# Two graph-attention layers on one core: layer 2 takes layer 1's tile scheme, and its normalization moves from POOL to DVE and ACT

## What is computed

```python
def _gat_layer(h, mask, b):
    scores = jnp.einsum('...nd,...md->...nm', h, h)
    scores = jnp.where(mask, scores, NEG)
    attn = jax.nn.softmax(scores, axis=-1)
    return jnp.einsum('...nm,...md->...nd', attn, h) + b
...
out_h = _gat_layer(h, mask[None, None], bh[None, :, None, :])      # H = 4 heads
z = jax.nn.leaky_relu(cat, negative_slope=0.2)
h2 = jnp.einsum('bnk,dk->bnd', z, Wo)
out2 = _gat_layer(h2, mask[None], bo)
z2 = jax.nn.leaky_relu(out2, negative_slope=0.2)
mu = jnp.mean(z2, axis=-1, keepdims=True)
var = jnp.mean(jnp.square(z2 - mu), axis=-1, keepdims=True)
out = (z2 - mu) * jax.lax.rsqrt(var + LN_EPS) * gamma + beta
...
x = _layernorm(x + _L1_gnn_ref(...), axis=-1)
```

## Time and profile before

| | |
|---|---|
| Median of three runs | 3392.47 us (3391.7 to 3395.71) |
| The profiled execution | 3385.7 us |
| Its span, first to last instruction | 3384.0 us |
| Mean granted TensorE clock | 0.964 |
| PE busy | 3073.0 us (91%) |
| DVE busy | 2755.6 us (81%) |
| ACT busy | 2336.7 us (69%) |
| POOL busy | 2600.1 us (77%) |

### The profile page before, as it was taken

The page is one execution under the profiler, slowest core; times in us unless marked ns, Lnnn a source line. Parts: engine busy times, 40 slices in busy tenths (PEclk is TensorE's granted clock), DMA queues, the critical chain, the costliest instruction groups (busy, mean ns, idle before and its releaser), DMA issues. The chain is left out here.

```text
span 3384.0 us, 126835 instructions
## 1 busy us (share of the span) xinstructions
PE 3073.0 (91%) x49399; PEld 2298.0 (68%) x49399; DVE 2755.6 (81%) x5040; ACT 2336.7 (69%) x2678; POOL 2600.1 (77%) x1891
## 2 busy tenths in 40 slices
PE   4874679999999999999999999999996599999997
PEld 3433457777777777777777777777765477777775
DVE  5477668888888888888888888888876599999998
ACT  1003557777777777777777777777765488888886
POOL 1026968999999999999999999999986337676775
PEclk7886989999999999999999999999998899999998
DMA  5103679998999999899999999999976623333331
GB/s 204 64 0 124 233 172 159 174 178 161 163 181 171 162 178 176 163 172 179 167 166 175 174 163 175 178 161 167 180 135 202 207 105 142 125 139 130 142 127 72
DMA packets 1195556, 528.52 MB, mean 156 GB/s; under 512 B 1091998, under 2 KB 1149788, under 8 KB 1192988
## 3 DMA queue, kind: packets, MB, share of 16 engines
q1 hardware_dynamic: 1193964, 518.57, 73.0%
q0 software_dynamic: 1200, 3.93, 0.3%
HBM read 123.09 MB, written 62.91 MB: 55 GB/s over the span
## 5 line engine op out<-in xcount | busy, mean ns | idle before, releaser
L627 POOL TENSOR_TENSOR mask_slot<-probs 128x1024 f16<-128x1024 f32 x1024 | 1915.7, 1893 | 209.5 <-ACT probs L984 123.0
L984 ACT ACTIVATE probs<-scores,shifted_max 128x2048 f32<-128x2048 f32 x512 | 1026.1, 2004 | 171.2 <-DVE shifted_max L1191 167.3
L1186 DVE CUSTOM_DVE_ANT_0 scores<-ps,mask 128x1024 f32<-128x1024 f32 x512 | 627.1, 1225 | 259.9 <-PE ps L842 255.3
L841 PE MATMUL ps<-operands 128*128 128x512 f16 x2048 | 778.7, 380 | 15.8 <-DMA v_parts<-h_d 15.1
L842 PE MATMUL ps<-operands 128*128 128x512 f16 x2048 | 778.0, 380 | 0.0
L989 ACT COPY probsT<-ps 128x1024 bf16<-128x1024 bf16 x512 | 518.1, 1012 | 360.9 <-PE ps L850 360.9
L1186 DVE CUSTOM_DVE_ANT_0 scores<-ps,mask,neg_max 128x1024 f32<-128x1024 f32 x512 | 657.4, 1284 | 93.3 <-issue 66.3
L850 PEld LDWEIGHTS ps<-ident,probs 128*128 128x128 bf16 x8192 | 515.8, 98 | 283.8 <-issue 145.9
L850 PE MATMUL ps<-ident,probs 128*128 128x128 bf16 x8192 | 624.2, 219 | 6.8 <-DVE probsT L1195 4.9
L861 PE MATMUL ps<-v_parts,probsT 128*128 128x64 f16 x8192 | 547.6, 193 | 0.0
L860 PE MATMUL ps<-v_parts,probsT 128*128 128x64 f16 x8192 | 547.2, 193 | 0.0
(11 more groups left out here) (171 smaller groups left out, 4640.1 us busy)
## 6 DMA issues: line engine op xcount, KB each, us to landing
mask_slot<-mask SPq DMA_DIRECT2D x129, 512.0 KB, 2.9
operands<-hT_d SPq DMA_DIRECT2D x160, 256.0 KB, 4.1
operands<-hT_d SPq DMA_DIRECT2D x40, 512.0 KB, 4.7
v_parts<-h_d SPq DMA_DIRECT2D x40, 512.0 KB, 5.0
scores<-in_adj SPq DMA_DIRECT2D x16, 1024.0 KB, 4.8
h_d<-outs SPq DMA_DIRECT2D x32, 512.0 KB, 2.8
hT_d<-probs SPq DMA_DIRECT2D x32, 512.0 KB, 2.8
probsT<-mask_slot SPq DMA_TRANSPOSE x1024, 3.9
```

What stands on the lines that cost most here:

```text
L627: pool.tensor_tensor(low[:, u, w], probs[:, u, w], high[:, u, w], ALU.subtract).then_inc(sem(f"low{half}"), 1)
L841: pe.matmul(ps[:, b, :], k_both[:, p, t * P:(t + 1) * P], q_head[:, p, w], start=True, stop=False)
L984: act.activation(probs[:, 1 - u, :], scores[:, 1 - u, :], ACT.Exp, bias=shifted_max[:, 1 - u:2 - u], scale=-1.0, accum_out=row_sum[:, held ...
L1186: dve.tensor_tensor_reduce(scores[:, u, w], ps[:, 2 * c:2 * c + 2, :].rearrange("p a n -> p (a n)"), mask[:, t * N + c * 2 * BANK:t * N + ...
```

## The change

Layer 2 runs through layer 1's step, now called `tile_step`, with `second` true: bf16 high part transposed by PE, low part subtracted on POOL and transposed by DMA, mask read from SBUF directly. `attention`, `step` and the staged mask go. The operands lie in two buffers: `hi_lo` (high above low), which serves as weights too, and `lo_hi` (low above high); this holds for layer 1 as well and makes four DMAs of 1.5 MB together.

The output of layer 2 gets its bias while it is copied, tile by tile. The normalization of instance i-1 and that of i-2 (its second part) run beside instance i, one piece per tile, on DVE and ACT. One chain of Newton steps on DVE at tile 13 makes the roots for both. Beta is added to x1 by POOL in the stage between. SP stores the output. Behind the last tile the pieces of the last two batches run by themselves (`after_layer2`), with the last scalings on DVE.

```diff
-        q_head = operands[:, 0]
-        q_tail = operands[:, 1]
-        k_both = operands[:, 2]
+        hi_lo = operands[:, 0]
+        lo_hi = operands[:, 1]
...
-                if k == 5:
+                if k == 3:
...
-                to, half, part, rows_ = ((q_head, 0, 0, D), (q_tail, 0, 1, D), (k_both, 0, 0, P), (q_head, 1, 0, D), (q_tail, 1, 1, D))[k]
+                to, row, at, rows_ = ((hi_lo, 0, 0, P), (lo_hi, 0, D, D), (lo_hi, D, 0, D))[k]
...
-            sp.dma_start(mask_slot[:, 0, :], mask[:, 0:N]).then_inc(sem("mask_staged0"), 16)
-
-            attention(LAYER1, INSTANCES, sp, step, 2 + OPERAND_DMAS)
...
+            unrolled(sp, tile_step, LAYER1, B)
+            after_layer2(finish)
+            sp.wait_ge(sem("out_stored"), 16 * B)
...
+                if w == 3:
+                    pool.tensor_tensor(by_tile(x1_of(b)), by_tile(x1_of(b)), parameter(3), ALU.add).then_inc(sem("beta_added"), 1)
...
-                            pe.matmul(ps[:, b, :], k_both[:, p, t * P:(t + 1) * P], q_head[:, p, w], start=True, stop=False)
+                            pe.matmul(ps[:, b, :], hi_lo[:, p, t * P:(t + 1) * P], hi_lo[:, p, w], start=True, stop=False)
...
-            attention(LAYER1, INSTANCES, act, step, 4)
+            unrolled(act, tile_step, LAYER1, B)
+            after_layer2(finish)
```

ACT's pieces (`i` is the instance under way, `p` its buffer, `tail` true behind the last tile):

```diff
+                if t == 7 and ends(i - 2):
+                    act.wait_ge(sem("f_centred2"), nth(i - 2))
+                    gate(act, "act")
+                    act.square(scratch2[:, :], x1_of(i - 2 - LAYER1)).then_inc(sem("f_squared2"), 1)
+                if t == 10 and ends(i - 1):
+                    act.wait_ge(sem("f_centred"), nth(i - 1))
+                    act.square(scratch[:, :], outs[:, 1 - p, :]).then_inc(sem("f_squared"), 1)
+                if t >= 14 and ends(i - 1) and not tail:
+                    if t == 14:
+                        act.wait_ge(sem("f_rstd"), nth(i - 1))
+                    scale_tiles(outs[:, 1 - p, :], ln[:, 4, :], *((0, 6) if t == 14 else (6, 11)))
+                if t == 0 and ends(i - 2) and (not tail or i == INSTANCES):
+                    scale_tiles(outs[:, p, :], ln[:, 4, :], 11, 16).then_inc(sem("f_scaled"), 1)
+                if 1 <= t < 4 and ends(i - 3) and (not tail or i == INSTANCES):
+                    scaled = scale_tiles(x1_of(i - 3 - LAYER1), ln[:, 5, :], *((0, 6), (6, 11), (11, 16))[t - 1])
```

DVE's output copy and its pieces, which stand at the end of the tile's step; waits and semaphores of the later ones are cut:

```diff
+                    if second:
+                        for tt in range(4 * k, 4 * k + 4):
+                            added = dve.scalar_tensor_tensor(outs[:, held, tt * D:(tt + 1) * D], out_slot(tt), row_inv[:, held, tt:tt + 1],
+                                                             rows[:, 1, :], ALU.mult, ALU.add)
...
+                if ends(i - 1):
+                    if t == 5:
...
+                        dve.scalar_tensor_tensor(y, y, 0.2, y, ALU.mult, ALU.max).then_inc(sem("f_leaky"), 1)
+                    if t == 8:
...
+                        dve.tensor_reduce(ln[:, 0, :], by_tile(y), AX.X, ALU.add).then_inc(sem("f_sum"), 1)
+                        dve.wait_ge(sem("f_sum"), n)
+                        dve.tensor_scalar(ln[:, 0, :], ln[:, 0, :], -1.0 / D, None, ALU.mult).then_inc(sem("f_mean"), 1)
+                    if t == 9:
...
+                        dve.tensor_tensor(by_tile(y), by_tile(y), over_features(ln[:, 0, :]), ALU.add).then_inc(sem("f_centred"), 1)
+                    if t == 12:
...
+                        dve.tensor_reduce(ln[:, 2, :], by_tile(scratch[:, :]), AX.X, ALU.add).then_inc(sem("f_ssq"), 1)
...
+                if t == 13 and (ends(i - 1) or ends(i - 2)):
+                    inverse_roots(n)
+                if ends(i - 2):
...
+                    if t == 1:
...
+                        dve.tensor_tensor(by_tile(y), by_tile(y), parameter(2), ALU.mult).then_inc(sem("f_gamma"), 1)
+                    if t == 2:
...
+                        dve.tensor_tensor(x1, x1, y, ALU.add).then_inc(sem("f_added"), 1)
+                    if t == 4:
...
+                        dve.tensor_reduce(ln[:, 1, :], by_tile(x1), AX.X, ALU.add).then_inc(sem("f_sum2"), 1)
...
+                    if t == 6:
...
+                        dve.tensor_tensor(by_tile(x1), by_tile(x1), over_features(ln[:, 1, :]), ALU.add).then_inc(sem("f_centred2"), 1)
+                    if t == 10:
...
+                        dve.tensor_reduce(ln[:, 3, :], by_tile(scratch2[:, :]), AX.X, ALU.add).then_inc(sem("f_ssq2"), 1)
...
+                then(dve.tensor_scalar(r.bitcast(I32), v.bitcast(I32), -0.5, 1597463007.0, ALU.mult, ALU.add))
+                for k in range(3):
+                    then(dve.tensor_tensor(newton[:, :], v, r, ALU.mult))
+                    then(dve.tensor_tensor(newton[:, :], newton[:, :], r, ALU.mult))
+                    then(dve.tensor_scalar(newton[:, :], newton[:, :], -0.5, 1.5, ALU.mult, ALU.add))
+                    root = dve.tensor_tensor(r, r, newton[:, :], ALU.mult)
+                    if k < 2:
+                        then(root)
```

More of the change, by code:

```diff
@@ L116, in pair, with unrolled @@
             return ap.rearrange("p (b c) -> p b c", c=D)
[L123 to L152 removed]
+        def unrolled(eng, step, first, count):
+            second = first == LAYER1
             def run(i, p, fresh=False):
@@ new lines, in by_tile, with over_features, parameter, x1_of @@
+        def by_tile(ap):
+            return ap.rearrange("p (t c) -> p t c", c=D)
+        def over_features(ap):
+            return ap.rearrange("p (t o) -> p t o", o=1).to_broadcast([P, NT, D])
+        def parameter(k):
+            return rows[:, k:k + 1, :].to_broadcast([P, NT, D])
+        def x1_of(b):
+            return col(xs, b, NT * D)
+        def ends(i):
+            return not isinstance(i, int) or LAYER1 <= i < INSTANCES
+        def nth(i):
+            return i - LAYER1 + 1
@@ L375, in _, with after_layer2 @@
+        def after_layer2(finish):
+            for t in range(FLUSH, NT):
+                finish(INSTANCES, t, 0, True)
+            for t in range(NT):
+                finish(INSTANCES + 1, t, 1, True)
+            for t in range(6):
+                finish(INSTANCES + 2, t, 0, True)
         @block.sync
@@ L484, in layer1_step, with finish @@
                     load_part(i + 1, 1 - p, k)
-                if t == 10 and not (isinstance(i, int) and i == 0):
+                if t == 10 and not second and not (isinstance(i, int) and i == 0):
                     store_z(i - 1, 1 - p)
+                if second:
+                    finish(i, t % NT, p)
+            def finish(i, t, p, tail=False):
+                if t == 5 and ends(i - 3):
+                    b = i - 3 - LAYER1
+                    sp.wait_ge(sem("f_done"), b + 1)
+                    gate(sp, "sp")
+                    sp.dma_start(out[b].rearrange("(p t) c -> p (t c)", t=NT),
+                                 x1_of(b)).then_inc(sem("out_stored"), 16)
             def load_z(b, w):
@@ L822, in layer1_step, with tile_step @@
-            def layer1_step(g, i, t, p, back):
+            def tile_step(g, i, t, p, back, second):
                 u = t % 2
@@ L989, in layer1_step, with finish, scale_tiles @@
                     act.copy(highT[:, u, N // 2:N], high_bank(1)).then_inc(sem("high_copied1"), 1)
-            unrolled(act, layer1_step)
+                if second:
+                    finish(i, t % NT, p, t >= NT)
+            def finish(i, t, p, tail=False):
+                def scale_tiles(v, rstd, first, end):
+                    for tt in range(first, end):
+                        scaled = act.activation(v[:, tt * D:(tt + 1) * D], v[:, tt * D:(tt + 1) * D], ACT.Copy, scale=rstd[:, tt:tt + 1])
+                    return scaled
+                if t == 7 and ends(i - 2):
[13 more added lines that the diff above has]
+                    scaled = scale_tiles(x1_of(i - 3 - LAYER1), ln[:, 5, :], *((0, 6), (6, 11), (11, 16))[t - 1])
+                    if t == 3:
+                        scaled.then_inc(sem("f_done"), 1)
+            unrolled(act, tile_step, 0, LAYER1)
             def copy_zT(k, u):
```

371 lines of the change are left out of this document (92 added, 279 removed).

## The result

The changed kernel took 3371.82 us (median of 4, 3368.04 to 3374.07) against 3392.09 (3389.44 to 3395.71) for the kernel before: a ratio of 0.9938 [0.9921, 0.9956]. It is 0.6% faster, 20 us. I had forecast 3402 us, 0.3% slower: the sign was wrong, the time inside the range.

A forecast was written before the change was run, and what follows sets the result against it. PE bounded both layers before, with DVE nearly full in layer 2; DVE would set layer 2 afterwards. The terms -5 + 3 - 9 + 7.5 + 2 + 11 = +9.5 us gave 3402 us; range 3325 to 3435.

The forecast's parts named there:

- The start of layer 2: Before layer 2's first mask: lighter operand loads and no wait for the staged mask row, together -9 us.
- The tail: From the last output copied to the end: two whole batches left unfinished, 33 us instead of 22.7, +11 us.
- From the last mask to the last output copied: After the last tile: 11.9 us instead of 9.5, +2 us.
- Instance: 74.8 + 3.4 + 4.4 + 2.2 + 1.2 = 86.0 us: 16 layer 2 tiles: DVE's work, pass waits, Newton's waits, PE's clock loss, two light steps set by PE.
- 661 forecast for layer 2: Layer 2: instances of 65, 81 and six at 86, less 1; against 653.5 before, +7.5 us.
- own range of the forecast: Whole kernel: 3380 to 3425 us, from 83 to 89 us an instance and the ends of other terms; chance 0.6.
- rival 1: Layer 2, tile 13: the waits hardly happen, an instance takes 76 us, the whole about 3335 us, faster; chance 0.25.
- Rival 2: Layer 2: a waiting DVE instruction always waits for both POOL halves, the whole about 3459 us; chance 0.15.
- Rival 3: Layer 1: operand loads were its limit, so -13 us instead of -5, the whole 3394 us; no chance given.
- -5: Layer 1: fewer operand loads shorten PE's wait for transposed data, -5 us (ends 0 and -13).
- -4.2: Start of layer 2: DVE's last copy waits 16.8 us behind operand loads; a quarter less gives -4.2 us.
- The stage between: Between the layers: POOL's eight additions of beta cost +3 us (ends 0 and 16).

The follow-up runs named there:

- two small repairs: Changed kernel with Newton's intermediates in PSUM and beta's additions taken out of the stage between: 3329.78 us, 0.9836 of the kernel before.

## Why the prediction failed

**What held.** DVE, not PE, sets layer 2 and fills 91% of it. The waits are where the text put them: in instructions that read SBUF twice, at tiles 1 to 9, and in Newton's chain at tile 13, with two of about 2 us one after the other; PE's clock falls once an instance. Moving the operands to PSUM removes them in the chain, and taking POOL's reads away leaves 0.14 us in one `tensor_scalar` of each chain. Reductions beside POOL's reads take 1207 to 1210 ns, while a `tensor_scalar` takes 1.81 and 0.67 us in place of 0.18. The Trainium skill, page SBUF — State Buffer, section Who interferes with whom, says that reductions never contend and that a `tensor_scalar` in its two-port mode can. The trace agrees in both. The start of layer 2 came as summed (-10.1 for -9, in the parts -5 and -5). The tail did too (+9.5 for +11), but in part by luck: its two chains took 2.9 us each and not 4.5, and from the end of the last scaling to the end of the span went 5.5 us and not 3. From the last mask to the last output copied it got slightly worse than forecast (+4.1 for +2).

**The step that failed** is the term "Instance: 74.8 + 3.4 + 4.4 + 2.2 + 1.2 = 86.0 us". It is 81.3 to 82.3. Its mechanism was right and its size 4.3 us off, six times, which is 26 of the 31 us between the 661 forecast for layer 2 and the 630.3 measured; the other 5 are the second instance (76.4 for 81), for the same reasons, the first (63.8 for 65), and the 1 us taken off for what follows the last mask. It has two parts:

- Tiles 13 to 15 took 20.1 us; the sum has 22.9 for them (12.4, 4.04, and 3.44 + 0.8 for output copies + 2.2). I had the thirteen instructions at 4.5 us by a spacing of 0.345 from the 0.32 of the earlier trace rows; they start 0.22 to 0.23 apart, 2.9 in all. Why that pair had more was not tried. The waits of the chain were 3.8 and not 4.4. Tile 14 took 3.4, DVE's own time, and not the 4.04 of PE, whose scores were ready. PE stood for 4.6 us, not for about 8, but the clock then cost what I had charged: tile 15 takes 6.4 in the mean, 2.2 more than without the roots, where PE never stands so long.
- The other thirteen tiles took 61.6; the sum has 63.0. The largest piece is gamma at tile 1: the tile took 5.0, while the sum had 6.2 (3.44 + 0.1 + 1.14 + a wait of 1.5). The rest is small differences over a dozen tiles.

The own range of the forecast (83 to 89 an instance) did not reach 82. The margin of 1.5 us an instance that rival 1 named as the point of decision is less than the error in the chain's spacing alone (4.5 - 2.9).

**Rival 1** named the right point (below 84.5 an instance the whole is no slower) for a wrong reason: the waits do happen, 7 us of them, as the run in which POOL only writes shows. **Rival 2**, that DVE waits for both halves each time, is refuted: the longest pass is 1.75 us over its shortest, less than one of POOL's instructions (1.9), and in the chain DVE and POOL take turns. **Rival 3**, that the loads were a limit for layer 1, is not shown by the length of layer 1; the loads did gain more than forecast:

**The loads** were the second error, in the terms "-5" for layer 1 and "-4.2" in the start of layer 2. Alone they give 0.63% (21 us), as much as the whole change. The traces place 9 us of it: 5 at layer 2's start, and 4 ahead of layer 1, where the same mechanism stands (PE's first product, and DVE's first mask behind it, wait for operand loads: 11.5 us, not 15.1) and where I hadn't looked. PE's waits for transposed data, which were to shrink, don't tell the two apart: 4.7 to 13.6 us in the nine executions with four loads, 6.4 to 15.3 in the four with the loads of before. The length of layer 1 varies by 16 us over the traces, by 10 over three of the kernel before, and the remaining 12 us can't be seen in it. Bytes alone don't explain them, since two loads of 4 KB take back more than half of the gain; where they lie stays open.

**The stage between** took +9.2, not +3, about half way to the end of 16. I had priced an addition at 1.89 us and taken POOL to have room for eight. They take 3.34 each, the products and leaky passes beside them get longer, and POOL is full (97.6 of 100 us). Apart from the products, beta costs about nothing (116.0, 112.6, against 111.3 to 114.6 before).

So, by the traces, what the change brings beside the loads is: staged mask -5, stage between +9, layer 2 -23, end +14, in all -5. Timed it is -1 (0.9935 with it, 0.9937 without, both on two buffers) or -8 (0.9977 on three), and those two agree within their intervals. The gain of the new layer 2, of which so much is written above, about pays for its tail and its beta. And its -23 is nowhere in the full instances: it comes from the two first ones (-19.6) and from the stalls (-12.7), whose cause no run here shows. I had compared 661 with 653.5 as a sum, which held those stalls, without noting that the usual instance before was 80.5.

## What to carry to other kernels

When a chain of small dependent instructions runs beside an engine that reads SBUF without pause, price it by its spacing and by one wait for each of the neighbour's instructions that it overlaps; then put its intermediates in PSUM, and the waits go while the spacing stays (6.7 to 3.2 us here, and more than half of what PE's clock cost behind it). Before giving an engine more work in a stage, add it up with the longer durations that the collision brings: eight additions filled POOL. Split a large change into its parts before believing its sum: here the two operand buffers alone gave as much as the whole change, and the large part needed two small repairs (1% together) before it gave more than 0.2%. Compare the steady instance with the steady instance, and count separately those at the edges and the ones with a stall.

## What was unexpected of the hardware

- Dependent DVE instructions of 32 columns start 0.22 to 0.23 us apart, in SBUF as in PSUM, each with a wait for the one before.
- In Newton's chain the waits alternate: for two POOL instructions in a row, two DVE instructions in a row wait once each (1.90 and 1.81), not one for both. In the stage between both engines lose: POOL's products go from 2127 ns to 3104 when beta's additions stand between them, DVE's leaky pass from 1297 to 1884 (medians).
- A `tensor_scalar` of 32 columns with one operand waits too (1.81 us) when both its ends are in SBUF; with both in PSUM it takes 0.20 beside the same reads.
- Layer 1 took 2108 to 2118 us in three executions of the kernel before, and 2104 to 2120 over all kernels.
- After 4.5 to 4.6 us without work PE was granted 0.50 of its clock, for its next 3 to 6 us.
